# Second layer's experts: picks in one block, their loop written out, one round of ranks, and a shared last gate/up tile

## What is computed

```
x_ffn = silu(xn @ gate_w.T) * (xn @ up_w.T) @ down_w.T      # gate_w, up_w: (682, 256)
```

```
scores = softmax(flat_x @ gate_w.T).T
topk_weight, topk_idx = top_k(scores, 256)
xg = flat_x[topk_idx]
eo = (gelu(xg @ Wg[e].T) * (xg @ Wu[e].T)) @ Wd[e].T * topk_weight
out = zeros.at[topk_idx].add(eo) + shared
```

## Time and profile before

| what | value |
|---|---|
| median of 3 runs | 3098.6 us (3097.91 to 3101.81) |
| the profiled execution | 3103.52 us |
| its span | 3101.4 us |
| PE busy | 2724.7 us, 88% of the span |
| DVE busy | 1527.6 us, 49% |
| ACT busy | 1143.9 us, 37% |
| POOL busy | 685.1 us, 22% |

### The profile page before, as it was taken

The page is one execution under the profiler, slowest core; times in us unless marked ns, Lnnn a source line. Parts: engine busy times, 40 slices in busy tenths (PEclk is TensorE's granted clock), DMA queues, the critical chain, the costliest instruction groups (busy, mean ns, idle before and its releaser), DMA issues. The chain is left out here.

```text
span 3101.4 us, 45194 instructions
## 1 busy us (share of the span) xinstructions
PE 2724.7 (88%) x16753; PEld 1598.9 (52%) x16793; DVE 1527.6 (49%) x2470; ACT 1143.9 (37%) x1973; POOL 685.1 (22%) x368
## 2 busy tenths in 40 slices
PE   7779998999989998999959878988988988599997
PEld 4265434753275425653348753452543533488886
DVE  5575355842774266733621145456454554743442
ACT  4673244532462255433312225345344343011110
POOL 0264044801562054602420100000000000022222
PEclk8889998999989998999979969999999899699999
DMA  5530002100120003000179710100100102044442
GB/s 187 228 146 15 1 1 107 42 1 0 62 81 8 1 1 121 29 1 1 68 260 328 267 28 8 21 18 4 22 21 1 22 7 89 14 142 145 163 163 63
DMA packets 63051, 223.56 MB, mean 72 GB/s; under 512 B 12565, under 2 KB 28394, under 8 KB 45578
## 3 DMA queue, kind: packets, MB, share of 16 engines
q1 hardware_dynamic: 46522, 191.62, 17.0%
q0 software_dynamic: 9760, 19.28, 2.6%
q10 hardware_dynamic: 6576, 10.05, 0.9%
HBM read 176.72 MB, written 39.99 MB: 70 GB/s over the span
## 5 line engine op out<-in xcount | busy, mean ns | idle before, releaser
L603 PE MATMUL psum<-arena 128*128 128x256 f32 (+6 forms) x4784 | 1255.7, 413 | 87.0 <-ACT arena L1467 11.5
L603 PEld LDWEIGHTS psum<-arena 128*128 128x128 f32 x4784 | 791.8, 198 | 484.5 <-issue 341.1
L2448 POOL TENSOR_TENSOR arena<-arena 128x1024 f32<-128x1024 f32 x128 | 299.4, 2365 | 137.2 <-DVE arena L1914 120.8
L1914 DVE TENSOR_TENSOR_SCAN arena<-arena,psum 128x512 f32<-128x512 f32 x256 | 291.5, 1201 | 49.7 <-PE psum L749 48.2
L749 PEld LDWEIGHTS psum<-arena 128*128 128x128 f32 x2048 | 240.6, 196 | 68.0 <-DVE arena L1914 43.6
L749 PE MATMUL psum<-arena 128*128 128x128 f32 x2048 | 252.1, 282 | 22.9 <-ACT arena L1490 22.9
L2480 POOL DMA_INDIRECT arena<-xn,arena x36 | 35.6, 988 | 978.8 <-DVE arena L2386 925.2
L2455 POOL TENSOR_TENSOR arena<-arena 128x1024 f32<-128x1024 f32 x32 | 76.0, 2374 | 671.5 <-ACT arena L1576 671.5
L2208 DVE TENSOR_REDUCE arena<-psum 128x1 f32<-128x512 f32 x256 | 163.0, 685 | 84.2 <-PE psum L1195 71.1
L1994 DVE SCALAR_TENSOR_TENSOR arena<-psum,arena 128x1024 f32<-128x1024 f32 x128 | 157.0, 1245 | 80.5 <-PE psum L886 80.1
L1742 ACT ACTIVATE arena<-psum 128x256 f32<-128x256 f32 x128 | 49.2, 384 | 377.6 <-PE psum L603 377.6
(11 more groups left out here) (295 smaller groups left out, 3049.2 us busy)
## 6 DMA issues: line engine op xcount, KB each, us to landing
arena<-in_W SPq DMA_DIRECT2D x46, 1024.0 KB
arena<-c_rows SPq DMA_DIRECT2D x32, 512.0 KB, 3.7
arena<-in_Wg SPq DMA_DIRECT2D x16, 1024.0 KB, 4.7
arena<-in_Wu SPq DMA_DIRECT2D x16, 1024.0 KB, 7.2
arena<-in_Wd SPq DMA_DIRECT2D x16, 1024.0 KB, 9.5
arena<-dl_all SPq DMA_DIRECT2D x5, 1024.0 KB, 5.1
arena<-duT_all SPq DMA_DIRECT2D x5, 1024.0 KB, 7.2
arena<-ut_all SPq DMA_DIRECT2D x5, 1024.0 KB, 9.1
```

The costliest lines, as they stand in the source:

```text
L603: r = mm(dst, w, x, start=i == 0, stop=i == len(pairs) - 1)
L1914: V.tensor_tensor_scan(hs[n % 3][:, c, :], dA[n % 2][:, c, :], bank[4 + c], 0.0, ALU.mult, ALU.add)\
L2448: nc.gpsimd.tensor_tensor(h, h, c_all[:, n % CBUFS, :].unsqueeze(1).broadcast_to([P, 2, L]), ALU.mult)\
```

## The change

It has three parts.

1. **Last gate/up tile.** The 42 last columns of gate and the 42 last of up share one stationary tile (gate in columns 0 to 63, up in 64 to 127). There is one projection less in each round. ACT's last silu reads partitions 0 to 63 and writes 64 to 127; DVE multiplies there. PE waits for up tile 4 only before the down projection, and for the shared tile (`last_gu`) before the last stationary tile of each down sum.
2. **Routing.** The search loop is written out, and the update of `thr` moves behind the comparisons of the next turn. Above and equal are ranked together in one pass: one pair of matmuls over 512 columns, one scan of 512, and the sum of both gives the slot.
3. **Experts.** The loop is written out. The roles in the pick matmul are swapped: 8 value columns are stationary, the one-hot (256 columns, now 16 buffers) moves, and four chunks go to four column groups of the array. All 16 picks of expert n + 1 stand in one block behind gate/up tile 2 of expert n; ACT copies the four partial sums (`keep_parts`), PE adds them behind tile 4 with two small matmuls (`gather_parts`), and DVE takes them behind product 5. There are no copies `idx_u` and `w_keep` any more: indices and weights have two buffers, so `take_picks(e)` waits for the scatter of e - 2 (`added`). POOL gathers one expert ahead instead of two. The transposes stand between the two halves of the down projection, whose first half waits for the last three products one by one. The last expert makes no picks.

```
-        w_g, w_u, w_d = take(KD, KF * P), take(KD, KF * P), take(KF, D)
+        w_g, w_u, w_d = take(KD, KF * P), take(KD, (KF - 1) * P), take(KF, D)
...
                 for m in range(KF):
                     project(LA, "gate", m, w_g, xn)
-                    project(LV, "up", m, w_u, xn)
-                dve_has("up", KF)
+                    if m < KF - 1:
+                        project(LV, "up", m, w_u, xn)
+                dve_has("up", KF - 1)
                 for m in range(2):
-                    project(LV, "down", m, w_d, gu)
+                    t = LV.fill(pe, b, "down", m)
+                    for k in range(KF - 1):
+                        mm(t, w_d[:, k, m * P:(m + 1) * P], gu[:, k, :], start=k == 0, stop=False)
+                    w(last_gu, 1)
+                    mm(t, w_d[64:P, KF - 1, m * P:(m + 1) * P], gu[64:P, KF - 1, :], start=False, stop=True)
...
-            with dve.Fori(0, 15) as i:
+            for i in range(15):
...
-                V.tensor_tensor(thr, thr, keep, ALU.bitwise_or).then_inc(bit_step.sem, 1)
                 V.tensor_tensor(cand, below, over(keep, s3k, 1), ALU.bitwise_or).then_inc(bit_step.sem, 1)
...
-            ranks(0, gt)
...
-            ranks(1, eq)
...
-            ranks(2, gt)
...
+            ind, slots = [v.rearrange("p (e x c) -> p c x e", c=CH, x=2) for v in (ind16, pre1)]
+            for x, op in enumerate((ALU.is_gt, ALU.is_equal)):
+                V.tensor_tensor(ind[:, :, x, :], sc, thf, op).then_inc(e_ind.sem, 1)
...
+            link(e_step, V.tensor_tensor_scan(incl1, const[:, C_SEG16:C_SEG16 + 2 * E1 * CH], bank[1], 0.0, ALU.mult, ALU.add))
...
+            link(e_step, V.tensor_tensor(pre1, incl1, bank[0], ALU.add))
+            V.memset(bank[0], 0.0).then_inc(picks_clear.sem, 1)
+            V.tensor_copy(sum4[:, 0:8], const[:, C_SUM4:C_SUM4 + 8])
+            link(e_step, V.scalar_tensor_tensor(pre1, pre1, 1.0, ind16, ALU.add, ALU.mult))
+            link(e_step, V.scalar_tensor_tensor(slotm[:, :, 0:E1], slots[:, :, 0, :], -1.0, slots[:, :, 1, :], ALU.add, ALU.add))
...
+            def picks(e):
...
+                for c in range(CH):
+                    pe.wait_ge(oh_ready.sem, oh_ready.at(c + 1, e))
+                    o = 32 * (c % 4)
+                    mm(bank[0][o:o + 8, 0:2 * P], vals[:, c, e, :], onehot[c], start=c < 4, stop=c >= CH - 4)
...
+            for n in range(E1):
+                for m in range(KH):
...
+                    if more and m == PICK_AT:
+                        picks(n + 1)
+                    if more and m == PARTS_AT:
+                        gather_parts(n + 1)
+                for hf in range(2):
+                    for k in range(KH):
+                        if hf == 0 and k >= KH - 3:
+                            pe.wait_ge(he_ready.sem, he_ready.at(k + 1, n))
+                        r = mm(bank[6 + j][:, hf * D:(hf + 1) * D], h1[:, k, hf * P:(hf + 1) * P], wdb[j][:, k, :],
+                               start=k == 0, stop=k == KH - 1)
+                    if more and hf == 0:
+                        transpose_picked(n + 1)
...
+            def take_picks(e):
...
+                V.tensor_copy(picked, bank[1][:, 0:16].rearrange("p (a b) -> p a b", a=2)).then_inc(pick_step.sem, 1)
...
+                dve.wait_ge(pick_step.sem, pick_step.at(1, e))
+                if e >= 2:
+                    dve.wait_ge(added.sem, added.at(32, e - 2))
+                V.scalar_tensor_tensor(idx[j], picked[:, :, 1], float(P), picked[:, :, 0], ALU.mult, ALU.add)
...
+            for n in range(E1):
+                if n + 1 < E1:
+                    gather(n + 1)
+                pool.wait_ge(eo_ready.sem, eo_ready.at(1, n))
+                for hf in range(2):
+                    pool.indirect_dma_start(out, on(ap=idx[n % 2][:, hf:hf + 1], axis=0), eo[n % 2][:, hf, :], None,
+                                            compute_op=ALU.add).then_inc(added.sem, 16)
+                    pool.wait_ge(added.sem, added.at(16 * (hf + 1), n))
```

More of the change, by code:

```diff
@@ L62, in at, with later @@
         return rnd * self.per + (n + self.ahead)
-    def later(self, rounds):
+    def later(self, rounds, per=0):
         s = Sig.__new__(Sig)
-        s.sem, s.per, s.ahead = self.sem, 0, self.at(0, rounds)
+        s.sem, s.per, s.ahead = self.sem, per, self.at(0, rounds)
         return s
@@ L1962, in _ @@
                 V.tensor_tensor(xb, xb, hb, ALU.add)
-                for m in range(KF):
+                for m in range(KF - 1):
                     t = LV.take(dve, b, "up", m)
@@ L2332, in _ @@
                         .then_inc(cnt_ready.sem, 1)
-                V.tensor_tensor(below, over(thr, s3k, 1), over(bits_u[:, bass.ds(3 * i + 3, 3)], s3k, 2), ALU.bitwise_or)\
+                if i > 0:
+                    V.tensor_tensor(thr, thr, keep, ALU.bitwise_or).then_inc(bit_step.sem, 1)
+                step(0)
+                V.tensor_tensor(below, over(thr, s3k, 1), over(bits_u[:, 3 * i + 3:3 * i + 6], s3k, 2), ALU.bitwise_or)\
                     .then_inc(bit_step.sem, 1)
@@ new lines, in _, with one_hots @@
+            link(e_step, V.scalar_tensor_tensor(slotm[:, :, 0:E1], slots[:, :, 0, :], -1.0, slots[:, :, 1, :], ALU.add, ALU.add))
+            dve.sem_inc(e_route.sem, 1)
+            def one_hots(e, first, last):
+                for c in range(first, last):
+                    if e >= 1:
+                        dve.wait_ge(oh_used.sem, oh_used.at(c + 1, e - 1))
+                    V.tensor_scalar(onehot[c], const[:, C_IOTA:C_IOTA + 2 * P], slotm[:, c, e:e + 1], None, ALU.is_equal)\
+                        .then_inc(oh_ready.sem, 1)
@@ new lines, in take_picks, with take_tokens @@
+                dve.wait_ge(pick_step.sem, pick_step.at(3, e))
+            def take_tokens(e):
+                dve.wait_ge(xe_full.sem, xe_full.at(1, e))
+                V.tensor_copy(xg1T, bank[2].rearrange("p (k n) -> p k n", k=KD)).then_inc(xe_sb.sem, 1)
+            one_hots(0, 0, CH)
+            take_picks(0)
+            one_hots(1, 0, AHEAD)
+            take_tokens(0)
+            for n in range(E1):
+                j, more = n % 2, n + 1 < E1
+                for m in range(KH):
+                    if more and m < PICK_AT:
+                        one_hots(n + 1, AHEAD + m * (CH - AHEAD) // PICK_AT, AHEAD + (m + 1) * (CH - AHEAD) // PICK_AT)
+                    dve.wait_ge(ga_ready.sem, ga_ready.at(m + 1, n))
+                    if m == 0 and n >= 1:
+                        dve.wait_ge(dn_full.sem, dn_full.at(1, n - 1))
+                    V.tensor_tensor(h1[:, m, :], ga[m % 2], bank[3 + m % 3][:, 2 * P:4 * P], ALU.mult).then_inc(he_ready.sem, 1)
+                    if more and m == PARTS_AT + 1:
+                        take_picks(n + 1)
+                if more:
+                    take_tokens(n + 1)
+                if n + 2 < E1:
+                    one_hots(n + 2, 0, AHEAD)
+                dve.wait_ge(dn_full.sem, dn_full.at(1, n))
+                if n >= 2:
+                    dve.wait_ge(added.sem, added.at(32, n - 2))
+                for hf in range(2):
+                    V.tensor_scalar(eo[j][:, hf, :], bank[6 + j][:, hf * D:(hf + 1) * D], w_slot[j][:, hf:hf + 1],
+                                    None, ALU.mult).then_inc((we_free, eo_ready)[hf].sem, 1)
```

280 lines of the change are left out of this document (114 added, 166 removed).

## The result

The changed kernel takes 3074.7 us (median of 5 runs, 3071.7 to 3082.6) against 3098.6 for the kernel before: ratio 0.9921, 95% interval 0.9903 to 0.9938. The profiled execution took 3074.7 us with a span of 3072.9, 28.5 less than that of before.

| stretch | before | after | difference | forecast |
|---|---|---|---|---|
| to the search's first comparison | 2635.7 | 2621.8 | -13.9 | -13.0 |
| threshold search | 40.6 | 36.4 | -4.2 | -3.0 |
| ranks | 13.8 | 7.2 | -6.7 | -7.5 |
| first picks to the first gate tile | 12.0 | 12.6 | +0.6 | +0.9 |
| 16 experts | 380.6 | 377.5 | -3.1 | +35.1 |

What follows compares the result with a forecast made beforehand. TensorE bounds the experts, VectorE's dependent steps the stages from search to slots. The terms -13.0 - 3.0 - 7.5 + 0.9 - 1.4 - 2.7 + 39.2 sum to +12.5 us; against the median 3098.6 it said 3111 us, range 3102 to 3121.

Steps and rivals of the forecast that it cites:

- the experts' order on GpSimd: Experts 1 to 14: gather behind both scatters (starts 2.1 and 12.6 us), 26.5 us an expert with clock loss, +39 us.
- two signs: The prediction is wrong if gathers start before t = 14 us, or if the experts' period is below 25 us.
- The clock: Experts: half clock follows TensorE's idle gap before the transposes, 0 to 1.9 us more an expert, taken as 0.9.
- The clock holds: Rival: in the experts the gap costs only itself, 25.6 us an expert, 3098 us in all; chance 0.22.
- The scatter isn't held up: Rival: first scatter lands 4.65 us after its start, gather waits only for picks, 22.1 us an expert, 3049 us; chance 0.16.
- Shared tile: First layer's FFN: one projection less and a covered wait before the down tiles, 3.25 us a round, -13.0 us.
- Search: Threshold search: written-out loop and moved update save 0.29 us in some 11 turns, -3.0 us (bounds 0 and -4.3).
- Ranks: Ranks stage: 13.7 us becomes 6.2, with two strided comparisons at 0.6 us each, -7.5 us (-5.5 to -8.5).
- First picks: Before the first expert: sums go through two more hand-overs and a copy, +0.9 us (0 to +2).
- Picks in one block: Experts on TensorE: 16 picks cost 0.8 us, or 1.7 if the four column groups don't overlap; 0.9 taken.
- Expert work on PE: TensorE's work is 22.1 us an expert when nothing is late: -1.4 us for expert 0, -2.7 for expert 15.
- The third rival: Rival "More is lost": clock low twice as long or code fetched late, 27.5 us an expert, 3126 us; chance 0.10.

Runs made afterwards that it cites:

- a1: Changed kernel with three index and weight buffers, the gather issued behind the second scatter, ahead of the wait for its landing: ratio 0.9832 to the kernel before.
- a2: Changed kernel with weights loaded for the first two experts only, the other 14 computing with those: ratio 0.9809 to the kernel before.
- a3: Changed kernel with all the semaphore increments GpSimd kept between its DMAs in the kernel before put back: ratio 1.0045 to the kernel before.
- h3: a3 with 6 calls of matmuls, their result overwritten, while TensorE waits for the gathered tokens: ratio 0.9982 to the kernel before.
- e1: Changed kernel with SyncE sending the next weights only when the first scatter has landed: ratio 0.9940 to the kernel before.
- b3: Changed kernel with SyncE waiting for the second scaled half instead of the first before sending the next weights: ratio 0.9890 to the kernel before.
- c1: Kernel before with only the shared last gate/up tile of the first layer's FFN: ratio 0.9933 to the kernel before.
- d2: d1 with the first layer's last down tile read over all 128 rows, the upper 64 cleared: ratio 0.9834 to the kernel before.
- b1: Changed kernel with only the GpSimd count before each expert's first scatter put back: ratio 0.9988 to the kernel before.
- h2: Changed kernel with a small GpSimd multiply, no count, before the first scatter of experts 1 to 15: ratio 0.9965 to the kernel before.
- d1: a1 with each expert's scatters back to back and the last expert's first half scattered while TensorE makes the second: 3043.0 us, ratio 0.9819 to the kernel before.

## Why the prediction was wrong

**The step that failed** is the sentence "The weights are still released just ahead of the first scatter, so I keep 2.1 and 12.6", in the part on the experts' order on GpSimd, together with the aside "some counts of GpSimd less", to which it gave no price. The mechanism was right: the gather stands behind both scatters, the first scatter among the weights, and PE idles before the transposes; taking away either cause (a1, a2) frees it. The size was not: the scatter started at 1.6, the second at 10.6, and the period was 23.4 us. With the counts back in place (a3) the forecast's total comes true: 26.7 us an expert where 26.5 was said, and 0.45% slower (0.28 to 0.62) where 3111 against 3098.6 is 0.40%. That it is so close is partly luck, since a3 reaches it with 2.8 us of idle time and 1.8 of clock, and the forecast had the data 3.5 us late and 0.9 of clock. Part of that 3.5 was to be a late first down half, ending at 19 instead of 18.1, which didn't come in the changed kernel. Of the two signs by which the prediction was to be wrong one came, the period below 25 us; the gathers start at 15.3 and not before 14.

The term by its parts: the counts cost 0.57 us at the start of the scatter, 0.5 behind its landing, and the shift takes the scatter past a step of 0.7 to 0.9 us in its own landing; in a3 that made 1.7 us more of idle time. The clock is the other 1.4 to 1.8. The kernel before had all of that too, since its 10.45 us between the scatters held a count, and paid nothing for it, because its gather was two experts ahead. A number read where it lies off the path was carried unexamined onto the path.

**The clock** was given 0.9 us behind a gap that ended 3.5 us late. The mechanism is there (h3), but 12 of the 14 gaps that came were 0.8 to 1.5 us long, below any of the 13 stretches of 1.8 to 2.8 us on which the term rested, and the grant stayed at 1.00 behind all but the first. The price itself was low rather than high: 1.4 to 1.8 us at a gap of 2.8. "All 13 were followed by half clock" was also too strong a basis: of the 68 gaps of 1.98 to 3.2 us in the experiments 32 had the full clock behind them.

**The rivals.** "The clock holds" was right on the clock and wrong on the gap. "The scatter isn't held up" was wrong on its mechanism: the scatters are 9.0 us apart with weights and 4.3 without (a2, e1). Neither was near in time: 3098 is 23 us above the result, 3049 is 26 below. The Trainium skill (DMA: Bandwidth & Descriptors, Queues, rings and completion order), by whose turns between queues 128 KB would be served beside the weights, isn't borne out in that reading, even for a scatter that starts 0.25 us behind them (b3, 9.4 us). No run shows the turns themselves. What was missing is a rival between the two: the chain as forecast, but shorter by what the edit takes off GpSimd. Its arithmetic was at hand: the sign turned at 25.6 us, only 0.9 below the forecast's 26.5, and the prices of the chain came from code that the change rewrites.

**The other terms.** Shared tile: 13.9 against 13.0; the cover held (c1). The agreement is partly luck: the prediction knew nothing of the step to 64 rows, 0.5 us by the loads and 0.4 by d2, eight times, and the stage's end moves by up to 17 us from profile to profile. Search: 4.2 against 3.0, within its bounds; a turn fell from 2.65 to 2.75 us to 2.35, so the loop's end was worth a little more than the 0.29 taken. Ranks: 6.7 against 7.5, by the two strided comparisons at 1.2 us. First picks: +0.6 against +0.9. Picks in one block: 16 records in 0.54 us (2804.20 to 2804.74 in a PE timeline), so the four column groups do overlap, and better than the 0.8 that I took as the lower case. Expert work on PE: 22.1, as said (a1, a2). The third rival's 27.5 us give 3125 and not 3126, which changes nothing.

## What to carry to other kernels

When an edit moves a DMA chain onto the critical path, cost every instruction of its queue anew, semaphore increments and waits too; a spacing read while the chain was hidden contains costs that the edit may remove. Where the forecast of the sign rests on a fraction of a microsecond that repeats 14 times, a rival with the chain shortened by each removed step belongs beside it. Issue a gather as soon as its index is there and ahead of waits that don't concern it: one more index buffer was worth 0.9% here.

## What the runs showed of the hardware

- A semaphore increment on GpSimd ahead of a DMA delays it by about 0.5 us (0.64 to 1.21 us behind Wg in b1), as much as a small multiplication with its hand-over (h2, 0.42). In a1, with one wait more ahead of the scatter and no increment, it is 0.53.
- A scatter of 128 KB alone is followed by the next after 4.0 to 4.6 us (a2, and the last two experts of every run). One that starts 0.25 to 0.81 us behind the first of 3 MB of weights holds the next up until 9.6 to 9.9 us behind that one's issue; one that starts 1.06 to 1.21 us behind it, until 10.8 to 10.9 (means, counts taken off). Holding the weights back only moves the hold to the next scatter (e1).
- No idle gap of TensorE of up to 1.97 us ahead of the transposes was followed by a lower granted clock (58 gaps in nine profiles); of those of 1.98 to 3.2 us 36 in 68 were, and the 16 matmuls behind then mostly took 5.3 us and not 3.63. Gaps of 2.4 and 2.8 us on average brought the experts' mean to 0.96 and 0.95, and matmuls without use in the gap brought it back to 1.00 and the time down by 0.6% (h3).
- A comparison of 128x256 floats into a bf16 tile with a stride takes 1.2 us in the changed kernel (L2385). What part of it is the stride's was not tested.
- Two matmuls to a tile of 64 rows and back cost 0.4 us more than the same over 128 rows (d1, d2).
